# Values two steps behind their scores, and GpSimd zeroing probabilities above the diagonal in the first three chunks

## The reference, cut to what matters

```python
q = (queries @ Wq.T + bq).reshape(N, L, H, -1)
k = (keys @ Wk.T + bk).reshape(N, S, H, -1)
v = (values @ Wv.T + bv).reshape(N, S, H, -1)
sm = jnp.einsum('nlhd,nshd->nlhs', q, k) / math.sqrt(D)
causal_mask = jnp.triu(jnp.ones((L, S), dtype=bool), k=1)
sm = jnp.where(causal_mask[None, :, None, :], -jnp.inf, sm)
sm = jax.nn.softmax(sm, axis=-1)
attn = jnp.einsum('nlhs,nshd->nlhd', sm, v)
```

## Time and profile before

| | us |
|---|---|
| median of 3 runs (1637.99 to 1643.67) | 1640.15 |
| profiled execution, device time | 1633.79 |
| its span, first to last instruction | 1632.1 |
| PE busy (89% of the span) | 1455.1 |
| DVE busy (52%) | 853.9 |
| ACT busy (42%) | 677.6 |
| POOL busy (25%) | 408.6 |

### The profile page before, as it was taken

One profiled execution on the slowest core, in us unless ns is written; L12 is line 12 of the kernel. 1 busy time (PEld: TensorE's weight loads), 2 busy tenths in 40 slices (PEclk: granted clock), 3 DMA queues, 4 the chain that ended last, 5 costly groups with the idle time before them and its releaser, 6 DMA issues. The chain is left out here.

```text
span 1632.1 us, 25573 instructions
## 1 busy us (share of the span) xinstructions
PE 1455.1 (89%) x8638; PEld 872.3 (53%) x8640; DVE 853.9 (52%) x1938; ACT 677.6 (42%) x1108; POOL 408.6 (25%) x346
## 2 busy tenths in 40 slices
PE   5789999999998759999999997479999767999996
PEld 3433333333324439999999997213332433666664
DVE  5689899987743662222222223688886454211110
ACT  4234566677784313333233332326778231122222
POOL 0110000098930250111111111020000326037554
PEclk9889999999999988999999999759999878999998
DMA  5901506027235631329513311420100401246553
GB/s 180 266 15 37 147 21 171 32 91 244 84 111 166 223 141 21 103 74 231 121 25 101 108 26 32 143 63 22 40 22 3 141 25 47 81 97 161 131 136 48
DMA packets 104050, 160.39 MB, mean 98 GB/s; under 512 B 15624, under 2 KB 85276, under 8 KB 101791
## 3 DMA queue, kind: packets, MB, share of 16 engines
q1 hardware_dynamic: 68319, 100.46, 20.3%
q0 software_dynamic: 22528, 48.87, 12.4%
q10 hardware_dynamic: 13120, 10.01, 2.3%
HBM read 101.76 MB, written 58.20 MB: 98 GB/s over the span
## 5 line engine op out<-in xcount | busy, mean ns | idle before, releaser
L818 DVE TENSOR_REDUCE mxp<-psA 128x1 f32<-128x512 f32 (+4 forms) x532 | 325.7, 664 | 58.5 <-PE psA L674 43.8
L792 ACT ACTIVATE Pt<-psC 128x1024 f32<-128x1024 f32 (+4 forms) x296 | 256.5, 918 | 142.0 <-PE psC L707 73.1
L674 PE MATMUL psA<-Kst,Qst 97*128 97x512 bf16 (+4 forms) x896 | 262.5, 362 | 39.7 <-DVE mxp L818 11.1
L700 PE MATMUL psC<-Qst,Kst 100*128 100x512 bf16 (+4 forms) x848 | 219.8, 367 | 2.4 <-DMA Qst<-mT 1.1
L1760 PE MATMUL psA<-xTt,OT 128*128 128x128 f32 x1728 | 203.2, 278 | 4.5 <-issue 4.4
L674 PEld LDWEIGHTS psA<-Kst,Qst 97*128 97x128 bf16 x896 | 74.9, 99 | 247.2 <-DVE mxp L818 117.5
L1760 PEld LDWEIGHTS psA<-xTt,OT 128*128 128x128 f32 x1728 | 198.4, 194 | 10.4 <-issue 10.4
L818 DVE TENSOR_REDUCE mxpt<-psA 128x1 f32<-128x449 f32 x256 | 145.2, 619 | 27.4 <-PE psA L674 22.3
L1847 DVE SCALAR_TENSOR_TENSOR Qst<-psA,b,sil 128x128 f32<-128x128 f32 x216 | 64.2, 345 | 152.9 <-ACT sil L1821 152.9
L792 ACT ACTIVATE Ptt<-psC 128x1024 f32<-128x1024 f32 (+1 forms) x128 | 123.8, 1020 | 47.9 <-PE psC L700 47.5
L1712 POOL DMA_INDIRECT residual<-yv,lab x36 | 56.0, 1555 | 350.0 <-DVE yv L1859 283.3
(11 more groups left out here) (328 smaller groups left out, 1779.8 us busy)
## 6 DMA issues: line engine op xcount, KB each, us to landing
rows<-blank SPq DMA_DIRECT2D x4, 4386.0 KB, 18.6
OT<-L_w SPq DMA_DIRECT2D x8, 2048.0 KB, 7.8
mi<-mask POOLq DMA_DIRECT2D x16, 800.5 KB, 4.7
Qst<-q_parts SPq DMA_DIRECT2D x96, 128.0 KB, 2.8
Kst<-k_parts SPq DMA_DIRECT2D x12, 800.5 KB, 15.1
w<-L_w SPq DMA_DIRECT2D x8, 1024.0 KB, 11.0
wg<-L_w_gate POOLq DMA_DIRECT2D x16, 352.0 KB, 4.0
wu<-L_w_up POOLq DMA_DIRECT2D x16, 352.0 KB, 4.2
```

The source lines that it names most:

```text
L674: mmi = pe.matmul(out, Qst[0:KA, half[u] % QN, at:at + P], Kst[0:KA, h, k0:k0 + w], start=True, stop=diag is None and not masked)
L700: mmi = pe.matmul(psC[0:kw, n % 2, y * 512 + col:y * 512 + QC], Kst[0:KC, h, k0:k0 + kw], Qst[0:KC, half[u] % QN, at + col:at + QC], start ...
L792: act.activation(Pt[0:kw, n % SLOTS, :, col:QC], psC[0:kw, n % 2, :].rearrange("p (y t) -> p y t", y=2)[:, :, col:QC], ACT.Exp).then_inc(p ...
L818: dve.tensor_reduce(mxp[:, q, hs[0]:hs[0] + len(hs), pc], psA[:, place_of[("piece", n)] % AB, 0:len(hs) * w].rearrange("p (h k) -> p h k", ...
```

## The change

Four things, all in `attention`.

- In chunks 0, 1 and 2 of the causal layer the mask matmuls are left out of `score_pack`.
- In their place POOL runs one `affine_select` for each of the 96 packs, in `gpsimd` between `add_bias` and `beside`. It waits for the pack's exponential and writes zeros above the diagonal of a block of 2 by 128 columns (both heads), in place in `Pt`. It counts up a new semaphore, `below`.
- The value pack of such a step waits for `below` instead of `pr`.
- `LAG` is 2 and `Pt` has 6 slots instead of 4 wherever the attention is not the one with a full mask (so in the second layer's short variant, `Ptt`, too): PE issues the value packs of step i - 2 in step i, and ACT reads `psO` out one step later accordingly.

```diff
+            on_diagonal = [n for n in range(2 * len(STEPS)) if causal and UNITS[STEPS[n // 2][0]][0] < NC - 1
+                           and STEPS[n // 2][2] >= UNITS[STEPS[n // 2][0]][0] * QTC]
+            zeroed_by = {n: i + 1 for i, n in enumerate(on_diagonal)}
...
+            SLOTS, LAG = (4, 1) if masked else (6, 2)
...
             def gpsimd(pool):
                 add_bias(pool)
                 if not masked:
+                    for n in on_diagonal:
+                        u, _, j = STEPS[n // 2]
+                        kw, col = tiles[j][1], first_column(UNITS[u][0], j)
+                        block = Pt[0:kw, n % SLOTS, :, col:col + P]
+                        pool.wait_ge(pr, n + 1)
+                        pool.affine_select(out=block, in_=block, compare_op=ALU.is_ge, fill=0.0, base=0,
+                                           pattern=[[0, 2], [1, P]], channel_multiplier=-1).then_inc(below, 1)
                     if beside is not None:
                         pool.wait_ge(pv, 2 * step0[max(u for u in range(NU) if UNITS[u][0] == NC - 2)])
                         beside(pool)
...
-                                        start=True, stop=not (masked or (causal and j >= s * QTC)))
+                                        start=True, stop=not (masked or (causal and j >= s * QTC and n not in zeroed_by)))
...
-                        elif causal and j >= s * QTC:
+                        elif causal and j >= s * QTC and n not in zeroed_by:
                             mmi = pe.matmul(psC[0:kw, n % 2, y * 512 + col:y * 512 + col + P],
                                             identb[0:kw, 0:kw], causbT[0:kw, :], start=False, stop=True)
...
-                    pe.wait_ge(pr, n + 1)
+                    if n in zeroed_by:
+                        pe.wait_ge(below, zeroed_by[n])
+                    else:
+                        pe.wait_ge(pr, n + 1)
...
-                    if i:
+                    if i >= LAG:
                         for b in range(2):
-                            value_pack(i - 1, b)
+                            value_pack(i - LAG, b)
...
-                for b in range(2):
-                    value_pack(len(STEPS) - 1, b)
+                for i in range(len(STEPS) - LAG, len(STEPS)):
+                    for b in range(2):
+                        value_pack(i, b)
...
-                    if i and group_no[i - 1] != group_no[i]:
-                        read_out(i - 1)
+                    if i >= LAG and group_no[i - LAG] != group_no[i - LAG + 1]:
+                        read_out(i - LAG)
```

More of the change, by code:

```diff
@@ L43 @@
 NV = DH + 1
-SLOTS = 4
 AB = 3
@@ L572, in attention @@
             o_free = sem(f"a{tag}_out_read")
+            below = sem(f"a{tag}_below_diagonal")
             chain = sem(f"a{tag}_chain")
```

## The result

The changed kernel takes 1650.24 us (median of 6 runs, 1645.92 to 1653.37) where the kernel before takes 1639.07 on the same chip (6 runs, 1629.95 to 1643.67): a ratio of 1.0073, 95% interval 1.0047 to 1.0098, slower by 11 us. Forecast were 1653 and +12.7. The profiled execution took 1646.22 us with a span of 1644.5.

The account below looks back on a forecast made before the run. PE and DVE by turns, with ACT, set the barrier, POOL having 45 us to spare. Barrier 521.4 + 5 - 8 + 1.2 = 519.6 against 508.9, +10.7; +2 of clock gives +12.7: 1640.15 + 12.7 = 1653 us, range 1643 to 1664.

Parts of the forecast that it names:

- POOL's order: Mask counting queued behind the 96 selects starts at 378.3, not 319.8, and ends at 521.4, 13.7 us behind the attention's end.
- loads late: Mask loads meet SP's blank-row stores once counting starts later: net 5 us lost, bounds -2 and +8.
- chunks 0 to 2: Leaving out 192 mask matmuls on PE saves 8 us there, range 5 to 12.
- clock behind the barrier: After standing still some 19 us, PE starts behind the barrier mostly at 1.2 GHz: 2 us lost, 0 to 7.
- The masks' two thirds: Of a 12 us ceiling for the mask matmuls on PE, 8 us saved, since DVE's idle time exceeds the masks.
- Cost: nothing: The second step of lag and 6 slots keep slot distances, and SP's later query loads have steps to spare: no time lost.
- PE's total is the same, here and in the second layer: The longer lag and extra slots leave PE's total unchanged in both layers' attention.
- Without the second step of lag the select would stand between the exponential and the values: In diagonal steps the extra step, 2.7 us on average, covers two selects needing under 1.4, at no PE cost.
- The shared port: Selects blocking DVE's two-input SBUF operations: some 3.4 us by the rule for six chains, under 1 us by the trace row.
- DVE did not keep the pace: Rival, chance 0.15: the masks' time turns into PE waiting for DVE, only 2 us saved; +18.7, 1659 us.
- The barrier did move: Rival, chance 0.10, said the barrier barely moves: whole ceiling saved, loads and clock 1 us each; +3.7, 1644 us.
- A mask matmul was worth: Faster rival, chance 0.04: PE loses 0.22 us on each mask matmul, its busy time; -13.1, 1627 us.

Follow-up runs that it names:

- quarter_count: The changed kernel, but POOL counts only 4 of the mask's 16 row tiles and multiplies the sum by 4; 1627.63 us, 0.996 of the kernel before.
- between_chunk2: The changed kernel, with 8 of the 16 counted tiles moved into POOL's free time between chunk 2's selects; 1629.98 us, 0.9929 of the kernel before.
- keep_masks: The changed kernel, with the mask matmuls of chunks 0 to 2 kept on PE beside the selects; 1657.63 us, 1.0139 of the kernel before.
- before_quarter: The kernel before, with POOL's counting cut to 4 of 16 tiles and the sum multiplied by 4; 1631.37 us, 0.9961 of the kernel before.
- lag_only_quarter: The kernel before with two steps of lag and 6 slots, and counting cut to 4 of 16 tiles; 1636.67 us, 0.9993 of the kernel before.
- lag_only: The kernel before with only the second step of lag and 6 slots: masks on PE, no selects, counting in its old place; 1652.03 us, ratio 1.0079.
- between_chunk2_lag1: The changed kernel with 8 tiles counted in chunk 2's pauses, but one step of lag and 4 slots; 1628.69 us, 0.9927 of the kernel before.

## Why the prediction was right, and where its terms were not

**POOL's order: right, and shown.** The barrier followed POOL's last addition. Counting cut to a quarter makes the kernel before 6.4 us faster (0.0039 of 1638.55) and the changed one 18.5 (1.0073 to 0.996); the 12 us between these are what the place of the counting costs. The two kernels with a quarter of the counting stand at the same ratio, 0.9961 and 0.996, so with so little counting the rest of the change is worth nothing that can be told (see **Open**, below). Moving the counting into chunk 2's pauses turns the loss into a gain.

**The sum, term by term**, in us of the profiled execution, predicted and measured:

| term | predicted | measured |
|---|---|---|
| first exponential | 0 | +1.1 (93.81 for 92.71: not the change) |
| order: counting begins behind the selects (521.4 - 508.9) | +12.5 | +12.5 |
| loads late | +5 | +7.1 (150.2 us of counting for 143.1) |
| chunks 0 to 2 | -8 | -10.5 |
| POOL's end to the barrier | +1.2 | +3.1 |
| sum at the barrier | +10.7 | +13.2 (522.15 for 508.92) |
| clock behind the barrier | +2 | +1.1 to the first projection matmul, +1.8 to the second layer's first exponential |

The mechanism held; the sizes were off in both directions and largely cancelled, so that the total came so close is in part luck. The order's term is the prediction's own on both sides; with it the measured rows add to 13.3. From the barrier on the profile is 0.8 us shorter than before, so the span grew by 12.4, where 12.7 was forecast. The clock's share is not shown apart: two kernels with the lag and no long pause, quarter_count and between_chunk2, stand at +2.3 and +2.4 where the changed kernel has +1.8. Two slips of the prediction's arithmetic moved nothing: its terms at their high ends add to +23.7, not +26 (the 1664 of the range fits the former), and two selects of 0.29 us take 0.58, not 0.56.

**Chunks 0 to 2.** The masks' two thirds, 8 us, met 6.4 by one pair of profiles (keep_masks). Chunk 2 alone gives the price more firmly: 124.1 us in each of the five profiles with two steps of lag and no masks, 127.4 in keep_masks, 127.5 in both profiles with masks and one step of lag (before, before_quarter). That is 3.3 us for 64 matmuls, 51 ns each and near the 60 of the prediction's rows, and next to nothing for the second step of lag (0.1 us with the masks, 0.4 without). The rest of the 10.5 us lies in chunks 0 and 1, where profiles of the same instructions scatter: 151.8 us in the changed kernel and 154.7 in between_chunk2, whose programs are alike up to chunk 1's last selects; 158.9 and 156.9 in before and before_quarter. With the masks and the lag it is 154.4 to 155.5 (lag_only_quarter, keep_masks, lag_only), without either 155.2 (between_chunk2_lag1). So "Cost: nothing" of lag and slots may have missed a gain of 1.4 to 4.5 us there, as far as this can be split.

**"PE's total is the same, here and in the second layer".** From its first exponential to its last read-out the short variant grew from 184.6 to 185.4 us, so that was close. What the lag was seen to cost is the clock behind the barrier, above; in the changed kernel that can't be seen, since the clock is at 0.50 there behind a pause of 17.5 us.

**"Without the second step of lag the select would stand between the exponential and the values".** Wrong as a reason: with one step of lag the kernel is as fast. PE's order alone, two score packs and some max pieces ahead of the values, covers a select of 0.41 us.

**The shared port.** Two figures stood beside each other: under 1 us by the row of 0.55 us, and 3.4 us, an estimate, if each of six chains waits for one whole select. Beside selects the price was small: none of the chain's operations took over 0.43 us between the first exponential and the last select. Where the step failed is that it asked only about the selects, and took the price from one row. That row was no small price but a late arrival, 2.77 us into a compare of 4.28:

```profile
335.00 4.28 POOL L1321 TENSOR_SCALAR mask_off<-mi 128x1601 bf16<-128x1601 int32 x1
```

```profile
337.77 0.55 DVE L833 TENSOR_TENSOR mparts<-zero,mx 128x16 bf16<-128x16 f32 x1
```

DVE's operation ends at 338.32, 0.96 us before the compare's end in the profile. In the first layer's attention, in all eleven profiles, each of the chain's 16 operations that a compare held up ends 0.95 to 0.97 us before the compare's end, and each that an addition or a select held up within 0.05 us of the end. So what a meeting costs is what is left of POOL's operation. The Trainium skill, "SBUF — State Buffer", section "SBUF: two separate sides", says that of a VectorE operation with two SBUF inputs and a GpSimd operation that reads SBUF, the one that starts first has the shared ports for its whole instruction and the other blocks. The trace agrees, but for those last 0.96 us of a compare. The trace of before had worse ones, ahead of the attention's first exponential, where POOL adds the bias in four operations from 76.96 to 86.6 and DVE's chain meets them:

```profile
80.82 0.94 DVE L833 TENSOR_TENSOR mparts<-zero,mx 128x16 bf16<-128x16 f32 x1
81.80 0.17 DVE L834 SCALAR_TENSOR_TENSOR mx<-mx,mparts 128x16 f32<-128x16 f32 x1
82.01 2.20 DVE L835 TENSOR_TENSOR mparts<-zero,mx 128x16 bf16<-128x16 f32 x1
```

The change moved the *counting*, whose operations are eight to ten times a select's length, to other chains. In the changed kernel:

```profile
416.62 2.57 DVE L849 TENSOR_TENSOR mparts<-zero,mx 128x16 bf16<-128x16 f32 x1
```

It lies within POOL's compare from 415.87 to 420.16 and ends 0.97 us before its end; PE then waited 2.25 us for a maxima buffer, and its clock was 0.50 from 421 to 426:

```profile
420.72 0.61 PE L686 MATMUL psA<-Kst,Qst 97*128 97x512 bf16 x1 [2.25 <-DVE mxp L834]
```

```profile
421.00:426.00 5.00, 5.00 (x16) 1.04 (x15) 2.27 (x5) 1.94 (x2) 4.67 (x3) 0.50 0.16 36
```

Group 1 of chunk 3 takes 39.8 us with this and 34.9 in quarter_count, which counts nothing beside it but its closing multiplication. That is most of why chunk 3 is 6.9 us longer, and why the attention ended at 505.3 and not near 500. It cost the changed kernel nothing, since POOL was last; in lag_only, where the attention is last, the same thing makes group 1 of chunk 3 9.7 us longer, in a profile that is 10.9 us longer in all.

**The rivals.** DVE did not keep the pace: its idle time took up the masks, though PE's weight loads wait for its buffers 89.4 us, 81.6 before. The barrier did move. A mask matmul was worth 33 ns (6.4 us / 192, the two profiles) to 51 ns (chunk 2), not its busy time of 224.

**Open.** before_quarter is 6.4 us faster than the kernel before, while both profiles have the barrier at 508.8 to 508.9. The profiles differ by 3.4 us, and 3.1 of it stands behind the second layer's attention, where other kernels show the same step with and without the lag; what sets it is not shown. The rest may lie in slower executions: the profiled execution of before was 5 us under its median here, and no slower one was profiled. quarter_count in turn reaches the barrier 9.7 us ahead of before_quarter, and its profile is only 2.8 us shorter: 2.7 us go up to the second layer's first exponential, 0.9 in its attention and 3.4 behind it. So an earlier barrier did not always give an earlier end, and a gain at the barrier is not the whole gain.

## What to carry to other kernels

When an engine gets new work, follow what was queued behind it to the next barrier: 38 us of selects in idle time cost 11 us, because they held back 143 us of counting whose slack was 45. If that work can be cut into pieces, put the pieces into the pauses between the new instructions, and choose the pauses by what runs beside them. Do not take one slow row for the price of a clash: look how much was left of the other engine's operation, and take its whole length as the worst case. And time a companion edit that looks free by itself: here the second step of lag was not needed, and alone, with the counting in its old place, it made the kernel slower.

## What was not expected of the hardware

- A two-input SBUF operation of DVE on 128 x 16 took 0.36 to 3.8 us beside POOL's compares and additions of 3.2 to 4.3 us, 0.17 to 0.19 without, by how much of POOL's operation was left. Where the two meet depends on shifts of a few us elsewhere: group 1 of chunk 3 took 43.9 us with two such meetings and 34.1 with none.
- Behind POOL's last instruction the barrier opens 3.11 us later in three kernels where POOL is last; behind ACT's last read-out 1.2 to 1.5 us.
- PE's granted clock behind the barrier differed (1.00 and 0.66) between two kernels whose pause there was the same within 0.06 us, and it stayed at 1.00 behind a pause of 2.15 us in a third.
